# Experts' scatters add into one row per node in DRAM, where two picked rows per node stood before

## The reference

```python
h = feats * rsqrt(deg_out)[:, None]
m = segment_sum(h[src], dst) * rsqrt(deg_in)[:, None]
x1 = m @ W_gc + b_gc + feats @ W_res + b_res
vals, idx = top_k(x1 @ Wg + bg, 2);  gates = softmax(vals)
for each expert e and each node that picked it (at most 1024 of them):
    core[node] += gate * (gelu(x1[node] @ w1[e] + b1[e]) @ w2[e] + b2[e])
y = x1 + core
mean, var = over all nodes, for each of the 256 columns
z = x + (y - mean) * rsqrt(var + 1e-5) * gamma + beta
out = (z - mean of row) / sqrt(var of row + 1e-5)
```

## Time and profile before

| | us |
|---|---|
| median of three runs | 3364.95 |
| lowest, highest | 3359.92, 3365.87 |
| the profiled execution | 3355.72 |
| its span in the profile | 3354.0 |

### The profile page before, as it was taken

How to read it: one execution, slowest core, us unless ns; L and a number is a source line. 1 busy time by engine, 2 the same in 40 slices (tenths; PEclk the granted TensorE clock), 3 DMA queues, 4 the chain that set the end, 5 groups by cost and what they waited for, 6 DMA issues and landing times. The chain is left out here.

```text
span 3354.0 us, 62238 instructions
## 1 busy us (share of the span) xinstructions
PE 2768.8 (83%) x15330; PEld 2088.9 (62%) x15478; DVE 2063.3 (62%) x7210; ACT 1246.9 (37%) x2967; POOL 2114.5 (63%) x2142
## 2 busy tenths in 40 slices
PE   5651399999989999989989999969999999999750
PEld 4530266666656666556656665539899989989640
DVE  7992155666666656666656666555555555555698
ACT  5981022222222222222222222224444444444339
POOL 5887377777777777777777777735555555555300
PEclk8875699999999999999999999989999999999885
DMA  7556745455554554555555545544444544444477
GB/s 246 150 169 202 257 145 174 146 165 156 166 170 142 169 175 143 168 175 148 165 160 162 169 141 168 166 131 132 159 137 148 165 139 132 146 145 134 140 296 250
DMA packets 331144, 557.86 MB, mean 166 GB/s; under 512 B 49199, under 2 KB 241997, under 8 KB 329314
## 3 DMA queue, kind: packets, MB, share of 16 engines
q0 software_dynamic: 101712, 273.85, 28.1%
q1 hardware_dynamic: 228942, 280.19, 25.0%
q10 hardware_dynamic: 324, 1.80, 0.2%
HBM read 428.12 MB, written 131.79 MB: 167 GB/s over the span
## 5 line engine op out<-in xcount | busy, mean ns | idle before, releaser
L1402 POOL DMA_INDIRECT work<-h_table,src_cols x1452 | 1379.6, 950 | 489.3 <-issue 474.5
L1803 PE MATMUL ps<-work 128*128 128x257 f32 x3322 | 1038.5, 395 | 160.9 <-DMA work<-h_table,src_cols 145.1
L1803 PEld LDWEIGHTS ps<-work 128*128 128x128 f32 x3322 | 581.9, 191 | 465.1 <-issue 326.3
L1675 PE MATMUL ps<-none_w,none 128*128 128x512 bf16 x1269 | 484.1, 381 | 0.0
L1949 POOL DMA_INDIRECT picked<-ys,places x228 | 251.1, 1101 | 352.1 <-DVE ys L2019 339.5
L2074 PEld LDWEIGHTS ps<-xst,work 128*128 128x128 f32 x3648 | 443.5, 192 | 28.4 <-issue 16.3
L2074 PE MATMUL ps<-xst,work 128*128 128x128 f32 x3648 | 447.4, 276 | 11.1 <-issue 10.4
L2081 PE MATMUL ps<-work,hid 128*128 128x256 f32 x1824 | 436.7, 382 | 1.4
L1930 ACT ACTIVATE hid<-ps,b_cols 128x128 f32<-128x128 f32 x912 | 315.6, 367 | 160.9 <-PE ps L2074 115.1
L2081 PEld LDWEIGHTS ps<-work,hid 128*128 128x128 f32 x1824 | 329.1, 190 | 47.2 <-ACT hid L1930 11.6
L1469 DVE TENSOR_TENSOR logits<-ps,gate_bias 128x64 f32<-128x64 f32 x98 | 22.0, 224 | 476.6 <-ACT acc L1357 476.6
(11 more groups left out here) (307 smaller groups left out, 4220.8 us busy)
## 6 DMA issues: line engine op xcount, KB each, us to landing
work<-in_L_gnn_w_dram SPq DMA_DIRECT2D x128, 512.0 KB
picked<-work SPq DMA_DIRECT2D x14, 1792.0 KB, 8.6
x_ahead<-work SPq DMA_DIRECT2D x182, 128.0 KB
work<-x_ahead SPq DMA_DIRECT2D x182, 128.0 KB, 2.7
pk<-picked SPq DMA_DIRECT2D x13, 1792.0 KB, 10.7
work<-h_table,src_cols POOLq DMA_INDIRECT x1452, 2.8
acc<-m_base SPq DMA_DIRECT2D x14, 903.0 KB, 6.6
x_beta<-xr_x SPq DMA_DIRECT2D x98, 128.0 KB
```

What stands on the lines that cost most here:

```text
L1402: pool.indirect_dma_start(out=got[:, c % RING, 0:D], out_offset=None, in_=h_table[:, :], in_offset=bass.IndirectOffsetOnAxis(ap=src_cols[: ...
L1675: nc.tensor.matmul(ps[:, 7, :], none[:, :], none_w[:, :], start=False, stop=False)
L1803: mm = nc.tensor.matmul(ps_flat[:, bank(t, k, w[0])], hot[:, (2 * t + (k >= HALF)) % HOTS, k % HALF if k >= HALF else k, :], got[:, c % RI ...
```

## The change

`picked` is gone, and so are the zero fills. In its place stands `y_rows`, one row of 256 floats for each node, 12.8 MB. `store` writes x1 to it beside `x1_rows`. The scatter adds (`compute_op=ALU.add`) its rows to what stands there. Since a node's two experts write to the same row, and nothing else orders them, GpSimd now waits for the scatter one turn back before it issues the next. The place is the node's row, so one operation on the table goes. The loop's end has no centring. `norms` loads y = x1 + core straight into `acc3`, all groups at once, since nothing in SBUF has to come free for it; VectorE only subtracts the mean. x + beta has a buffer of its own (`xb`) of eight groups, the squares of the row statistics go to `sq`, and the results are written in place and stored from `acc3`.

```diff
@@ aggregate
-                def clear_picked(q):
-                    rows = picked.rearrange("(p n r) d -> p n r d", p=P, n=SETS)[:, q, :, :]
-                    sp.dma_start(rows, got[:, RING, 0:D].unsqueeze(1).broadcast_to([P, TOP_K * SET, D])).then_inc(zeros_out, 16)
...
                 def store(a, b):
                     sp.wait_ge(gates_set, b)
                     sp.dma_start(by_lane(x1_rows)[:, a:b, :], acc3[:, a:b, :]).then_inc(rows_out, 16)
+                    sp.dma_start(by_lane(y_rows)[:, a:b, :], acc3[:, a:b, 0:D]).then_inc(rows_out, 16)
...
-                        sp.wait_ge(zeros_out, 16 * SETS)
...
-                    if slot == 0:
-                        sp.wait_ge(got_set, 4)
-                    if slot % SET == 2 and slot < NT:
-                        clear_picked(slot // SET)
...
-                sp.wait_ge(rows_out, 16 * (SETS - 1 + SET))
+                sp.wait_ge(rows_out, 32 * (SETS - 1 + SET))
...
-                nc.vector.scalar_tensor_tensor(place_of, row_of, float(TOP_K), second_of, ALU.mult, ALU.add).then_inc(table_set, 1)
+                nc.vector.tensor_tensor(place_of, row_of, first_of, ALU.add).then_inc(table_set, 1)
                 dve.wait_ge(table_set, 9)
-                nc.vector.tensor_tensor(place_of, place_of, first_of, ALU.add).then_inc(table_set, 1)
-                dve.wait_ge(table_set, 10)
                 nc.vector.scalar_tensor_tensor(first_of, place_of, float(BIG // 2), second_of, ALU.is_lt, ALU.subtract)
@@ experts
-                    pool.indirect_dma_start(out=picked[:, :], out_offset=bass.IndirectOffsetOnAxis(ap=places[:, u:u + 1], axis=0),
-                                            in_=ys[:, u, :], in_offset=None, bounds_check=PLACES - 1,
-                                            oob_is_err=False).then_inc(y_sent[u % 2], 16)
+                    pool.indirect_dma_start(out=y_rows[:, :], out_offset=bass.IndirectOffsetOnAxis(ap=places[:, u:u + 1], axis=0),
+                                            in_=ys[:, u, :], in_offset=None, bounds_check=ROWS - 1,
+                                            oob_is_err=False, compute_op=ALU.add).then_inc(y_sent[u % 2], 16)
...
                         if not isinstance(n, int) or n > 1:
                             pool.wait_ge(y_sent[u % 2], 32 * j + 16 * (u // 2))
                         pool.sem_inc(freed, 1)
+                        if not isinstance(n, int) or n > 0:
+                            pool.wait_ge(y_sent[(u + 1) % 2], 32 * j + 16 * ((u + 1) // 2))
+                            pool.sem_inc(carrier, 1)
                         send(n, u)
                         if u < fetches:
                             fetch(u)
...
-                dve.wait_ge(mean_set, 1)
-                for g in range(CENTRED):
-                    rows = acc3[:, g * GT:(g + 1) * GT, 0:D]
-                    nc.vector.tensor_tensor(rows, rows, y_total[:, :].unsqueeze(1).broadcast_to([P, GT, D]), ALU.subtract)
@@ norms
-        B = 4
+        B = 8
...
-        pk = t2("pk", [P, B, GT, TOP_K * D], F32)
+        xb = t2("xb", [P, B, GT, D], F32)
...
-                rows = picked.rearrange("(n k) d -> n (k d)", k=TOP_K)
-                for g in range(NG):
-                    if g == 0:
-                        for n, (a, b) in enumerate(FIRST_PARTS):
-                            sp.dma_start(pk[:, 0, a:b, :], by_lane(rows)[:, a:b, :]).then_inc(first_in[n], 16)
-                        continue
-                    if g >= B:
-                        sp.wait_ge(second_added, adds(g - B))
-                    sp.dma_start(pk[:, g % B, :, :], rows_of(rows, g)).then_inc(pk_in[g % B], 16)
-                    if g == B - 1:
-                        sp.dma_start(gamma_b[:, :], gamma.rearrange("(a d) -> a d", a=1).broadcast_to([P, D])).then_inc(gamma_in, 16)
-
                 def load_x(q):
-                    sp.dma_start(pk[:, held(q), :, D:2 * D], rows_of(x_beta, q)).then_inc(xb_in[held(q)], 16)
+                    sp.dma_start(xb[:, q % B, :, :], rows_of(x_beta, q)).then_inc(xb_in[q % B], 16)
...
                     if g < NG - 1:
                         sp.wait_ge(normed, GT * (g + 1))
-                        sp.dma_start(out[g * GT * P:(g + 1) * GT * P, :].rearrange("(t p) d -> p t d", p=P),
-                                     pk[:, held(g), :, 0:D]).then_inc(o_out[held(g)], 16)
+                        sp.dma_start(out[g * GT * P:(g + 1) * GT * P, :].rearrange("(t p) d -> p t d", p=P), group(g)).then_inc(o_out, 16)
...
+                for g in range(NG):
+                    for n, (a, b) in enumerate(parts(g)):
+                        sp.dma_start(group(g, a, b), rows_of(y_rows, g, a, b)).then_inc(landed(g, n), 16)
+                sp.dma_start(gamma_b[:, :], gamma.rearrange("(a d) -> a d", a=1).broadcast_to([P, D])).then_inc(gamma_in, 16)
                 for q in range(B):
-                    sp.wait_ge(second_added, adds(NG - B + q))
                     load_x(q)
...
                 def centre(g):
-                    nc.vector.tensor_tensor(group(g), group(g), mean[:, :].unsqueeze(1).broadcast_to([P, GT, D]),
-                                            ALU.subtract).then_inc(centred, 1)
-
-                def add(g, a, b, n):
-                    nc.vector.tensor_tensor(group(g, a, b), group(g, a, b), pk[:, g % B, a:b, 0:D], ALU.add).then_inc(first_added, 1)
-                    dve.wait_ge(first_added, n)
-                    nc.vector.tensor_tensor(group(g, a, b), group(g, a, b), pk[:, g % B, a:b, D:2 * D], ALU.add).then_inc(second_added, 1)
-
-                for g in range(CENTRED, UPFRONT):
+                    for n, (a, b) in enumerate(parts(g)):
+                        dve.wait_ge(landed(g, n), 16)
+                        nc.vector.tensor_tensor(group(g, a, b), group(g, a, b), mean[:, :].unsqueeze(1).broadcast_to([P, b - a, D]),
+                                                ALU.subtract).then_inc(centred, 1)
+
+                for g in range(NG):
                     centre(g)
-                done = 0
-                for g in range(NG):
-                    if g >= CENTRED:
-                        dve.wait_ge(centred, g - CENTRED + 1)
-                    if g > 0:
-                        dve.wait_ge(pk_in[g % B], 16 * (g // B + (g % B > 0)))
-                    for n, (a, b) in enumerate(FIRST_PARTS if g == 0 else parts(g)):
-                        if g == 0:
-                            dve.wait_ge(first_in[n], 16)
-                        done += 1
-                        add(g, a, b, done)
-                    if g + UPFRONT < NG:
-                        centre(g + UPFRONT)
-
-                dve.wait_ge(sq_used, NG - 1 + len(LAST_PARTS))
+
+                dve.wait_ge(sq_used, parts_until(NG))
...
-                    dve.wait_ge(xb_in[held(g)], 16 * (g // B + 1))
+                    dve.wait_ge(xb_in[g % B], 16 * (g // B + 1))
                     for u in range(GT):
-                        last = nc.vector.scalar_tensor_tensor(tile(g, u), tile(g, u), 1.0, pk[:, held(g), u, D:2 * D], ALU.mult, ALU.add,
+                        last = nc.vector.scalar_tensor_tensor(tile(g, u), tile(g, u), 1.0, xb[:, g % B, u, :], ALU.mult, ALU.add,
...
-                    if g >= B:
-                        dve.wait_ge(o_out[held(g)], 16 * (g // B))
                     for u in range(ON_ACT, GT):
-                        last = nc.vector.scalar_tensor_tensor(pk[:, held(g), u, 0:D], tile(g, u), z_mean[:, g % 2, u:u + 1], tile(g, u), ALU.add, ALU.mult,
+                        last = nc.vector.scalar_tensor_tensor(sq[:, g % 2, u, :], tile(g, u), z_mean[:, g % 2, u:u + 1], tile(g, u), ALU.add, ALU.mult,
...
                     if g >= 2:
-                        act.wait_ge(sq_used, g - 1)
-                    for n, (a, b) in enumerate(parts(g)):
-                        act.wait_ge(second_added, len(FIRST_PARTS) + g + n)
+                        act.wait_ge(sq_used, parts_until(g - 1))
+                    for a, b in parts(g):
+                        done += 1
+                        act.wait_ge(centred, done)
                         nc.scalar.activation(sq[:, g % 2, a:b, :], group(g, a, b), ACT.Square).then_inc(squared, 1)
...
-                    if g >= B:
-                        act.wait_ge(o_out[held(g)], 16 * (g // B))
                     for u in range(ON_ACT):
-                        last = nc.scalar.activation(pk[:, held(g), u, 0:D], tile(g, u), ACT.Square, bias=z_mean[:, g % 2, u:u + 1],
+                        last = nc.scalar.activation(sq[:, g % 2, u, :], tile(g, u), ACT.Square, bias=z_mean[:, g % 2, u:u + 1],
...
-                        nc.scalar.activation(pk[:, held(g), u, 0:D], tile(g, u), ACT.Identity, bias=shift[:, g % 2, u:u + 1],
+                        nc.scalar.activation(tile(g, u), tile(g, u), ACT.Identity, bias=shift[:, g % 2, u:u + 1],
                                              scale=rstd[:, g % 2, u:u + 1]).then_inc(normed, 1)
```

62 lines of the change are left out of this document (29 added, 33 removed).

## The result

The changed kernel takes 3650.38 us (median of four runs, 3648.2 to 3657.2) against 3364.81 of the kernel before on the same chip: a ratio of 1.0855, 95% interval [1.0839, 1.0871], slower. The prediction was 3551 with a range of 3385 to 3756 and 0.84 on slower: direction and range held, the sum was 100 us short. The profiled execution took 3648.2 us with a span of 3646.5, against 3355.72 and 3354.0.

The account below looks back on a forecast made before the run. GpSimd paces the edge stage, TensorE the expert loop, VectorE the norms' first half. The terms +217 - 4.2 - 26.4 - 0.7 = +186 us, added to the median 3364.95, gave 3551, range 3385 to 3756.

Parts of the forecast that it names:

- The loop: Expert loop: each scatter waits for the previous one's landing, so a turn is 4.87 us and 228 take 1110 against 893, +217.
- wake-up: GpSimd in the expert loop: time from a landing to the next scatter's start, 0.95 us with the new semaphore step.
- L: Adding scatter in the expert loop: start to landing, 3.5 us in a calm turn (2.8 + 0.7), mean 3.92.
- added by weight loads: Expert loop: landings beside weight loads are 1.5 us slower, in 28% of the turns, 0.42 us a turn.
- Hidden wait: Rival, expert loop: a landing of 2.3 us hides the wait and the loop stays; 3334 us, chance 0.13.
- Nearly plain: Rival, expert loop: the addition is free and a scatter lands in 2.8 us; loop 951, +58, total 3392, chance 0.17.
- Serial: Rival, expert loop: read and write one after the other, landing 5.1 us; loop 1475, +582, total 3916, chance 0.10.
- Norms at the low clock: Rival, norms' first half: TensorE stays at the low clock, -3 in place of -26.4, so 3574; no chance given.
- The loop's end: Between loop and norms: VectorE's three centring operations leave, GpSimd's last scatter is late next; -4.2 us.
- Norms, first half: VectorE loses 28 adds and half the centrings, TensorE is the next bound; 57.2 us in place of 83.6, -26.4.
- Norms, second half: Squares go to sq, results stay in place; the store waits that fall away never bound; 0, within 1 us.
- Edge stage: Zero fills go, 20 stores of y_rows come, GpSimd's pace feels neither: 0 within 3 us; VectorE's last chain -0.7 us.

Follow-up runs that it names:

- e1: The kernel before with the new wait alone: each plain scatter waits for the one before it; 3410.06 us, ratio 1.0138.
- e2: The kernel before with the addition alone: scatters add to the zeros of their own rows, two in flight; 3460.11 us, ratio 1.0282.
- e3: The kernel before with both addition and wait, in its own layout with two rows a node; 3685.86 us, ratio 1.0950.
- e6: The changed kernel with SyncE's loads of the later experts' weights cut to 16 lanes (wrong weights from the fifth expert on); 3524.21 us, ratio 1.0481.
- e10: The kernel before with the weight loads from the fifth expert on cut to 16 lanes, so later experts compute wrongly; 3331.54 us, ratio 0.9910.
- e7: The changed kernel with scatters that add only the first half of each row, 512 B, the other half left out; 3549.01 us, ratio 1.0549.
- e4: The changed kernel with the loop of before: plain scatters into a table nobody reads, no zero fills, addition or new wait; 3331.15 us, ratio 0.9901.
- e13: The kernel before with VectorE's operations on rows_at, places and gate moved ahead of its wait for TensorE's result; 3331.11 us, ratio 0.9920.

## Why the prediction was right, and which terms were off

**The loop, +217 predicted, +322 measured.** The mechanism was the one named: scatter n waits for the landing of n-1, the pace is landing plus wake-up, and GpSimd's 1.5 us of idle time is no room for it. e1, e2 and e3 show that both parts are needed, e6 that the landing sets the pace. Direction and mechanism were no luck; that the total stayed inside the range owes something to its width, as three terms erred the same way. The step that was mis-sized is L, and with it every factor around it, all in one direction:

| term, us a turn | predicted | measured | from | times 227 |
|---|---|---|---|---|
| calm landing | 3.5 | 3.75 | e6, mean | +57 |
| added by weight loads | 0.42 | 0.54 | after less e6, mean | +27 |
| wake-up | 0.95 | 1.03 | next start less landing | +18 |
| turns in which `ys` comes last, and the rest | 0 | 0.03 | 5.345 - 5.31 | +7 |
| one turn fewer, 227 between 228 starts | | | | -5 |

That is +104, and 322 - 217 is 105; the prediction also counted the loop of before from 893 us, where it is 891. For the calm landing I had taken a plain landing of 2.8, the gather's and so the upper end of the 2.3 to 2.8 that I had named, and added 0.7 for the second trip. A plain scatter lands after 2.5 to 2.6 (e10, e1), and the addition adds 1.2 to it, not 0.7: one error hid part of the other. The premise "it issues the same descriptors as a plain one" was false. GpSimd is 1.58 us at it in place of 1.0 to 1.1, and its queue carries 96 packets more a scatter. Of the 0.7, the 0.3 for the DRAM read's latency has no run that shows it alone. "A second read of the same bytes is some 0.4 more" can be set only beside e7: 64 KB cost 0.49, 128 KB some 1.0 (an estimate), for reading and writing together.

For the loaded turns the rows of the loop's start gave 1.5 us more, at 28% of the turns. A quarter of the landings in after (57) are of 4.46 us or more, with a mean of 5.96, which is 2.2 over a calm one; the one shown here is 6.13. The excess was taken too small and the share a little too large, and the product came out 0.12 short.

**The rivals.** Hidden wait needed a mean of L + 0.95 under 3.92; it was 5.3, and even a plain scatter with the new wait costs 46 us (e1). Nearly plain, 3392, falls by e1 against e3: with plain scatters the loop is 940.9 us, about the 951 of that rival, and the addition makes it 1222.0. Serial, L = 5.1, was too high by 1.35; how read and write share the 3.75 no run shows. Norms at the low clock did not come: a group took 3.2 us, and only the first, at 6.33, was slow.

**TensorE's clock in the loop.** "The cover of its full clock is not certain": it fell to 0.94 on the mean. As the landings pace the loop, it costs no more than the 8 us that they leave over.

**The loop's end, -4.2 against -3.7.** Wake-up again, and a landing of 3.8: 3488.75 to 3493.09 is 4.34, with 3.6 predicted.

**Norms, first half, -26.4 against -29.2.** Right, with TensorE as the next bound, and in size by errors of both signs. The prediction's 83.6 and 57.2 end before the variance chain, the table's 86.5 behind it; with the same 2.9 us the forecast was 60.1, and 57.3 was measured. First data came 2.8 us after the issue (the issue at 3493.09, VectorE's first subtraction at 3495.86) and not 4.1; its part is half as large, 256 KB. The groups took 3.2 and not 3.5 us. Against that the first group took 6.33 and not 5.3, and TensorE waited 2.25 us behind it. e4 shows the gain by itself.

**Norms, second half, 0 against 0.** Right.

**Edge stage, 0 within 3, and -0.7, against +3.25.** The table's operation went, the gathers end 4 us later (mean 953 ns in place of 950, 1452 of them). That is just outside the bound given. e4, with the same stores, starts its scatters late too (2279.7), but e1 at 2274.3 and e2 at 2279.3, with the edge stage of the kernel before, spread as much, so nothing here is put down to the stores.

**Traffic.** Written bytes fell by 12.85 MB as said. Read bytes were to rise by 12 and fell by 12.85: the forecast counted a read at the destination of each addition, and the page counts none. e2_add settles that it is the count: with the addition as its one edit it shows the bytes of before to the last digit, though each of its 228 scatters adds to what stands in DRAM:

```profile
HBM read 428.12 MB, written 131.79 MB: 162 GB/s over the span
```

**The landing by a fit.** By the fit of the Trainium skill, "DMA: Bandwidth & Descriptors", section on the anatomy of one DMA on the GpSimd path, a DMA of 128 KB lands after 2.3 us, an estimate. Plain scatters do about that, 2.1 at the least and 2.5 on the mean without the weight loads (e10); adding ones take 3.75. The same page of the Trainium skill, rules for kernel authors, says that the semaphore of an earlier accumulate must be waited for. That is what the wait is for: it has a price here, 1.0 us of wake-up and 3.75 us of landing a turn. No run here adds to shared rows without it, so none shows what would be lost.

**Left open.** What part of the addition's 1.2 us is GpSimd's longer work, the packets, or the read. Why fetches beside additions and weight loads land later than beside either alone (the one shown in e2 after 5.76 us). Whether the changed kernel gains from e13's move: its loop hardly waits for `ys`, so it should not, but it wasn't tried.

## What to carry to other kernels

Two edits that each look hidden can be dear together: price an added wait by the landing of the very transfer it waits for, and that landing with every other edit to it, then set landing plus wake-up against the turn. A wait for the transfer just issued turns a latency into a throughput; if transfers have to be ordered, change the layout so that they needn't be, as the two rows a node did. And where an engine waits for another in each turn, look at what stands behind that wait and doesn't need its result: moving it ahead gained 28 us here, nearly the 33 us that the change gained in the norms and at the loop's end.

## What the runs showed of the hardware

- An indirect scatter that adds in DRAM occupies GpSimd 1.58 us for 128 rows, whether they are of 1 KB or 512 B (e7); a plain one of 1 KB rows takes it 1.0 to 1.1.
- It lands after 3.75 us on the mean without weight loads beside it (e6), 4.28 with them (after); a plain one after 2.52 (e10) and 2.97 (e1).
- It moves in 128 packets of 1024 bytes, a plain one in 32 of 4096, and the profile's account of bytes read leaves out the read at its destination (e2 against before).
- Half the bytes take 0.49 us off its median landing of 3.83 (e7).
- From a landing to the start of the DMA that waits for it GpSimd needs 1.03 us, in 222 of the 227 turns of after no more than 1.1.
- On a 128x1792 tile VectorE's tensor_tensor with both inputs in SBUF takes 5.49 us in place of 2.02 while GpSimd does the same operation, which takes GpSimd 4.1.
- A plain scatter's time on GpSimd is 1.01 us in every row of e13's turns and 1.10 on the mean in the kernel before (251 us for 228). What VectorE does in the same moment differs between them; that this is the cause was not tested.
- TensorE's granted clock was 0.94 on the mean of a loop that left it idle for a fifth, granted at 0.50 for 3.4 us behind a turn in which it had idled 3 us, and 1.00 throughout the loop of before, where it was busy for 97%.
